# A fused early-fusion block: residual on VectorE, one gate/up bank ahead of the transposes, VectorE's feed-forward queue reordered, attention epsilons inside the sums

## What is computed

```python
h = patch_tokens(x)                        # (32, 36, 256): layernorm, product, layernorm
h = concatenate([h, txt], axis=1)          # (32, 113, 256)
h = h + attention(layernorm(h))            # differential attention, 8 heads, causal
h = h + ffn(layernorm(h))                  # fp4-quantised inputs and weights
# in attention, per head: q, k = rope(rmsnorm(.)); RMS_EPS = eps of float32
#   a = softmax(s[0]) - lam * softmax(s[1]);  out = layernorm(a @ v) * (1 - LAMBDA_INIT), LN_EPS = 1e-5
# in ffn: fp4_linear(silu(fp4_linear(x, w_gate)) * fp4_linear(x, w_up), w_down)
# fp4: per block of 16 elements a scale max|x|/6, then the nearest of 8 magnitudes, times the scale
```

## Time and profile before

| | |
|---|---|
| median of three runs | 659.81 us |
| the profiled execution | 662.52 us, span of its instructions 660.8 us |
| TensorE busy | 576.4 us, 87% |
| VectorE busy | 554.1 us, 84% |
| ScalarE, GpSimd busy | 322.1 us, 309.8 us |
| DMA | 48 GB/s over the span |

### The profile page before, as it was taken

One profiled execution on the slowest core, in us unless ns is written; L12 is line 12 of the kernel. 1 busy time (PEld: TensorE's weight loads), 2 busy tenths in 40 slices (PEclk: granted clock), 3 DMA queues, 4 the chain that ended last, 5 costly groups with the idle time before them and its releaser, 6 DMA issues. The chain is left out here.

```text
span 660.8 us, 14226 instructions
## 1 busy us (share of the span) xinstructions
PE 576.4 (87%) x3666; PEld 470.0 (71%) x3666; DVE 554.1 (84%) x1444; ACT 322.1 (49%) x760; POOL 309.8 (47%) x455
## 2 busy tenths in 40 slices
PE   5665568999999999999999998589999999999996
PEld 4554455767776776777677676478888888888885
DVE  5999847898889889888988985498888888888884
ACT  2242215655665665566565564244544444445442
POOL 2455523555455445545554553155455445545542
PEclk9878776999999999999999997789999999999999
DMA  6900000011111111111111101111111111111111
GB/s 173 325 17 23 24 16 18 27 38 41 30 40 35 35 35 38 40 34 37 35 41 29 42 23 46 30 39 49 48 54 52 54 48 54 49 48 48 57 32 35
DMA packets 33734, 31.99 MB, mean 48 GB/s; under 512 B 6098, under 2 KB 32050, under 8 KB 33714
## 3 DMA queue, kind: packets, MB, share of 16 engines
q1 hardware_dynamic: 33714, 31.75, 16.3%
...
## 5 line engine op out<-in xcount | busy, mean ns | idle before, releaser
L741 PE MATMUL bank<-v_sb,pt 113*113 113x33 f32 x1024 | 109.1, 262 | 0.0
L741 PEld LDWEIGHTS bank<-v_sb,pt 113*113 113x113 f32 x1024 | 108.4, 181 | 0.7 <-issue 0.7
L858 POOL TENSOR_SCALAR_AFFINE_SELECT pt<-pt 113x452 f32<-113x452 f32 x128 | 73.9, 600 | 68.5 <-ACT pt L798 68.5
L798 ACT ACTIVATE pt<-bank 113x452 f32<-113x452 f32 x128 | 63.1, 545 | 38.2 <-PE bank L729 38.2
L138 PE MATMUL bank<-wgu_hi,fx_hi 128*128 128x512 f32 x174 | 69.5, 399 | 8.0 <-DVE fx_lo L1131 8.0
L1177 POOL TENSOR_TENSOR h_deq<-fh,fhb 128x704 f32<-128x704 f32 x29 | 40.3, 1389 | 68.8 <-DVE fhb L1084 56.3
L729 PE MATMUL bank<-q_blk,k_t 64*113 64x452 f32 x256 | 67.7, 605 | 0.0
L138 PE MATMUL bank<-wgu_hi,fx_lo 128*128 128x512 f32 x174 | 66.8, 384 | 0.0
L138 PE MATMUL bank<-wgu_lo,fx_hi 128*128 128x512 f32 x174 | 66.7, 384 | 0.0
L138 PE MATMUL bank<-wqkv_hi,xo_hi 128*113 128x256 f32 (+1 forms) x128 | 50.3, 393 | 17.7 <-DVE xo_lo L923 17.7
L1191 POOL TENSOR_TENSOR fh<-fh,fhb 128x704 f32<-128x704 f32 x29 | 40.3, 1391 | 42.2 <-DVE fhb L1145 42.2
...
## 6 DMA issues: line engine op xcount, KB each, us to landing
...
```

The costliest lines, as they stand in the source:

```text
L741: mm = pe.matmul(pv_ps[s % 2][0:T, s // 2, :], pt[0:T, s, :], v_sb[0:T, s // 2, :], start=True, stop=True, skip_group_check=True)
L798: act.activation(pt[0:T, GS * g:GS * (g + 1), :].rearrange("p s t -> p (s t)"), sc_ps[g % 2][0:T, :], ACT.Exp, scale=1.0 / math.sqrt(HD)). ...
L858: pool.affine_select(out=grp, in_=grp, compare_op=ALU.is_ge, fill=0.0, base=0, pattern=[[0, GS], [1, T]], channel_multiplier=-1).then_inc( ...
```

## The change

It has three parts.

In attention, the epsilons go into the sums as one more element. `v_sb`'s last column, which gives the row sum, is set to sqrt(32 * LN_EPS) in place of 1, so that squaring z with 33 elements a head includes the epsilon. The squares are scaled by 1/HD and 1/VD within the Square, and the q/k squares have a 17th element that holds RMS_EPS. The copy of the row sums, `eps0`, `z_var` and `qk_var` go; `mix` has 4 semaphore steps in place of 5.

In the feed-forward, the residual is no longer multiplied in on TensorE. `rows_out` moves from ScalarE to VectorE and adds the residual `rb` to `down_ps`. Its load is issued one step later.

The queues of the feed-forward get another order: TensorE takes the first gate/up bank, then the transposes of the hidden row, then the other two banks; VectorE takes `x_maxima` and `x_inverse` first and `h_low` after `h_scales`, with `rows_out` at the end; GpSimd takes `x_quotient` ahead of `h_dequantise`; ScalarE `h_magnitude` ahead of `h_high`.

```diff
 LN_EPS = 1e-5
 RMS_EPS = float(np.finfo(np.float32).eps)
+SUM_COLUMN = math.sqrt(VD * LN_EPS)
 LAMBDA_INIT = 0.8 - 0.6 * math.exp(-0.3 * 4)
...
         hr = sb("hr", [P, D])
         xn = sb("xn", [P, D])
         xo_hi, xo_lo = sb("xo_hi", [P, 2 * KD, T], F32R), sb("xo_lo", [P, 2 * KD, T], F32R)
-        sq = sb("sq", [P, 2 * D])
-        ssq = sb("ssq", [P, 2 * SH])
+        sq = sb("sq", [P, 2 * SH, HD + 1])
         NV = 2 + NH + 2 * SH
...
@@ -790,7 +791,8 @@
             def squares(b):
                 act.wait_ge(m["qk_made"], b + 3)
                 after(act, m["qk_sums"], b + 2)
-                act.activation(sq[0:T, :], qk_ps[0:T, :], ACT.Square).then_inc(m["qk_squared"], 1)
+                act.activation(sq[0:T, :, 0:HD], blocks(qk_ps[0:T, :], HD), ACT.Square,
+                               scale=1.0 / math.sqrt(HD)).then_inc(m["qk_squared"], 1)
             def exps(b, g):
                 act.wait_ge(m["scores_made"], NG * b + g + 1)
...
             return steps
         def attention_vector(dve):
-            dve.memset(v_sb[:, :, VD:VD + 1], 1.0).then_inc(m["ones_set"], 1)
+            dve.memset(v_sb[:, :, VD:VD + 1], SUM_COLUMN).then_inc(m["ones_set"], 1)
+            dve.memset(sq[:, :, HD:HD + 1], RMS_EPS).then_inc(m["ones_set"], 1)
+            dve.memset(w1[:, :, VD:VD + 1], 0.0).then_inc(m["ones_set"], 1)
             dve.memset(var[:], 1.0).then_inc(m["ones_set"], 1)
             dve.memset(moments[:], 1.0).then_inc(m["ones_set"], 1)
-            dve.wait_ge(m["ones_set"], 3)
+            dve.wait_ge(m["ones_set"], 5)
             def newton_step(b):
...
                     dve.wait_ge(k["lambda_step"], 5)
                 dve.wait_ge(m["pv_made"], NG * b)
                 dve.reciprocal(rs_1[0:T, :], pv_ps[1][0:T, :, VD]).then_inc(m["mix_step"], 1)
-                dve.tensor_copy(s0[0:T, :], pv_ps[0][0:T, :, VD]).then_inc(m["mix_step"], 1)
-                dve.wait_ge(m["mix_step"], 5 * b - 3)
-                dve.scalar_tensor_tensor(ratio[0:T, :], s0[0:T, :], lam[0:T, :], rs_1[0:T, :], ALU.mult,
+                dve.wait_ge(m["mix_step"], 4 * b - 3)
+                dve.scalar_tensor_tensor(ratio[0:T, :], pv_ps[0][0:T, :, VD], lam[0:T, :], rs_1[0:T, :], ALU.mult,
                                          ALU.mult).then_inc(m["mix_step"], 1)
-                dve.scalar_tensor_tensor(eps0[0:T, :], s0[0:T, :], LN_EPS, s0[0:T, :], ALU.mult,
-                                         ALU.mult).then_inc(m["z_sums"], 1)
-                dve.wait_ge(m["mix_step"], 5 * b - 2)
-                dve.tensor_tensor(blocks(w1[0:T, :], VD), pv_ps[1][0:T, :, 0:VD], spread(ratio[0:T, :], VD),
+                dve.wait_ge(m["mix_step"], 4 * b - 2)
+                dve.tensor_tensor(w1[0:T, :, 0:VD], pv_ps[1][0:T, :, 0:VD], spread(ratio[0:T, :], VD),
                                   ALU.mult).then_inc(m["mix_step"], 1)
-                dve.wait_ge(m["mix_step"], 5 * b - 1)
-                dve.tensor_tensor(blocks(z[0:T, :], VD), pv_ps[0][0:T, :, 0:VD], blocks(w1[0:T, :], VD),
-                                  ALU.subtract).then_inc(m["mix_step"], 1)
+                dve.wait_ge(m["mix_step"], 4 * b - 1)
+                dve.tensor_tensor(z[0:T], pv_ps[0][0:T], w1[0:T], ALU.subtract).then_inc(m["mix_step"], 1)
             def z_sums(b):
                 dve.wait_ge(m["z_squared"], b)
-                dve.tensor_reduce(ssz[0:T, :], blocks(z2[0:T, :], VD), AXX, ALU.add).then_inc(m["z_sums"], 1)
-            def z_var(b):
-                dve.wait_ge(m["z_sums"], 2 * b)
-                dve.scalar_tensor_tensor(var[0:T, HEADS], ssz[0:T, :], 1.0 / VD, eps0[0:T, :], ALU.mult,
-                                         ALU.add).then_inc(m["z_var"], 1)
+                dve.tensor_reduce(var[0:T, HEADS], z2[0:T], AXX, ALU.add).then_inc(m["z_sums"], 1)
             def qk_sums(b):
                 dve.wait_ge(m["qk_squared"], b + 3)
-                dve.tensor_reduce(ssq[0:T, :], blocks(sq[0:T, :], HD), AXX, ALU.add).then_inc(m["qk_sums"], 1)
-            def qk_var(b):
-                dve.wait_ge(m["qk_sums"], b + 3)
-                dve.tensor_scalar(var[0:T, QK], ssq[0:T, :], 1.0 / HD, RMS_EPS, ALU.mult, ALU.add).then_inc(m["qk_var"], 1)
+                dve.tensor_reduce(var[0:T, QK], sq[0:T], AXX, ALU.add).then_inc(m["qk_sums"], 1)
             def residual(b):
@@ -997,7 +990,7 @@
                     between()
                 run(b, seq, (
                     (3, ln_sums), (-1, mix), (1, rope_sum), (-2, residual),
-                    (2, qk_sums), (-1, z_sums), (-2, out_sums), (-1, z_var), (2, qk_var),
+                    (2, qk_sums), (-1, z_sums), (-2, out_sums),
                     ((3, -2), variances)))
...
                 sp.dma_start(xb[:], h2_dram[bass.ds((t + 3) * P, P), :]).then_inc(f["x_loaded"], 16)
             def load_residual(t):
-                after(sp, f["r_added"], t - 1)
-                sp.dma_start(rb[:], h2_dram[bass.ds((t - 1) * P, P), 0:D]).then_inc(f["r_loaded"], 16)
+                after(sp, f["out_made"], t - 2)
+                sp.dma_start(rb[:], h2_dram[bass.ds((t - 2) * P, P), 0:D]).then_inc(f["r_loaded"], 16)
             def store(t):
                 rows = LAST if isinstance(t, int) and t - 2 == FT - 1 else P
@@ -1065,9 +1057,8 @@
             def steps(t):
                 if tile(t, 3):
                     load(t)
-                if tile(t, -1):
+                if tile(t, -2):
                     load_residual(t)
-                if tile(t, -2):
                     store(t)
...
             def scale(amax_of, dst, made):
                 dve.tensor_scalar(dst[:], amax_of, -1.0 / 6.0, -MIN_SCALE, ALU.mult, ALU.min).then_inc(f[made], 1)
+            def rows_out(t):
+                dve.wait_ge(f["down_made"], t - 1)
+                dve.wait_ge(f["r_loaded"], 16 * t - 16)
+                after(dve, f["stored"], 16 * t - 32)
+                dve.tensor_tensor(res[:], down_ps, rb[:], ALU.add).then_inc(f["out_made"], 1)
             def h_low(t):
                 dve.wait_ge(f["ht_high"], t - 1)
@@ -1160,9 +1158,9 @@
             def steps(t):
                 run(t, tile, (
-                    (-2, h_low), (-1, h_rounded), (-1, h_codes), (-1, h_scales), (2, x_maxima), (2, x_inverse),
+                    (2, x_maxima), (2, x_inverse), (-1, h_rounded), (-1, h_codes), (-1, h_scales), (-2, h_low),
                     (0, hidden), (1, x_low), (0, h_maxima), (0, h_inverse), (2, x_rounded), (2, x_codes),
-                    (2, x_scales)))
+                    (2, x_scales), (-2, rows_out)))
             return steps
@@ -1201,7 +1199,7 @@
             def steps(t):
                 run(t, tile, (
-                    (-1, h_dequantise), (2, x_quotient), (0, h_quotient), (2, x_dequantise)))
+                    (2, x_quotient), (-1, h_dequantise), (0, h_quotient), (2, x_dequantise)))
             return steps
@@ -1249,16 +1247,9 @@
                 act.activation(xa[:], xb[:, 0:D], ACT.Identity, bias=xb[:, D:D + 1],
                                scale=xb[:, D + 1:D + 2]).then_inc(f["x_normed"], 1)
-            def rows_out(t):
-                act.wait_ge(f["down_made"], t - 1)
-                after(act, f["stored"], 16 * t - 32)
-                act.activation(res[:], down_ps, ACT.Copy).then_inc(f["out_made"], 1)
             def steps(t):
                 run(t, tile, (
-                    (-2, h_high), (-1, h_magnitude), (0, silu), (1, x_high), (2, x_magnitude), (3, x_norm),
-                    (-2, rows_out)))
+                    (-1, h_magnitude), (-2, h_high), (0, silu), (1, x_high), (2, x_magnitude), (3, x_norm)))
             return steps
...
                 return split3(pe, gu_flat[:, cols], x_hi, x_lo, lambda k: wgu_hi[:, k, cols],
                               lambda k: wgu_lo[:, k, cols], KD)
-            def gate_up(t):
+            def first_columns(t):
                 if isinstance(t, int) and t == 0:
@@ -1282,6 +1273,8 @@
                 pe.wait_ge(f["xt_low"], t + 1)
                 after(pe, f["silu_made"], t)
                 columns(0)
+            def other_columns(t):
                 after(pe, f["hidden_made"], t)
                 columns(1).then_inc(f["gate_made"], 1)
                 columns(2).then_inc(f["up_made"], 1)
...
                     mm = pe.transpose(fxt_ps[:, k * P:(k + 1) * P], x_deq[:, k * P:(k + 1) * P], ident[:])
                 mm.then_inc(f["xt_made"], 1)
-            def residual(t):
+            def down(t):
                 if isinstance(t, int) and t == 2:
                     pe.wait_ge(m["h2_added"], NSEQ)
-                pe.wait_ge(f["r_loaded"], 16 * t - 16)
                 after(pe, f["out_made"], t - 2)
-                pe.matmul(down_ps, ident[:], rb[:], start=True, stop=False).then_inc(f["r_added"], 1)
-            def down(t):
                 pe.wait_ge(f["ht_low"], t - 1)
                 split3(pe, down_ps, lambda k: fh_hi[:, k, :], lambda k: fh_lo[:, k, :],
```

(4 more changed lines are left out.)

27 lines of the change are left out of this document (14 added, 13 removed).

## The result

| | before | after |
|---|---|---|
| median | 659.39 us (4 runs, 658.19 to 660.0) | **676.71 us** (4 runs, 675.53 to 678.23) |
| ratio | | **1.0266**, interval 1.024 to 1.0293 |
| profiled execution (span) | 662.52 (660.8) | 676.38 (674.6) |

Slower, as forecast, but by 2.7% where 1.0% was forecast: 676.7 lies outside the range of 660.5 to 671.5. The two spans differ by 13.8 us. From here on a timeline shows only the rows that bear on its reading.

The account below looks back on a forecast made before the run. Bound: in the feed-forward a 7.75 us VectorE-GpSimd-ScalarE ring, in attention TensorE's ring of 9.60. 26 x 0.20 + 27 x 0.02 + 1.6 - 0.8 = +6.5 us gave a median of 666.3, range 660.5 to 671.5.

Parts of the forecast that it names:

- The ring: Feed-forward tile: VectorE from h_rounded to h_inverse 5.00 us, then via GpSimd and ScalarE to h_rounded 2.75; closed at 7.75.
- TensorE as follower: Feed-forward: TensorE isn't a member of the 7.75 us ring; it waits for h_deq in the same tile.
- the residual: Feed-forward: moving it from TensorE to VectorE's rows_out, inside the wait for h_abs, was put at 0 us.
- The collision: Feed-forward: GpSimd's x_quotient runs across h_rounded's start and shuts it out, 0.20 us a tile in 26 tiles.
- no collision: Feed-forward rival: steps are off by 0.2 us or h_rounded gets in first; +1.3, 661.1 us; chance 0.14.
- full collision: Feed-forward rival: register waits or the loop's branch hold x_inverse back, 0.35 to 0.47 a tile; 670.2 to 673.3; chance 0.12.
- by the queue alone the period is 7.77: VectorE's feed-forward queue: 0.85 us out of the ring, 0.87 in; +0.02 a tile in 27 tiles.
- a rival for attention: Looped attention sequences gain up to 0.24 each, 6 us: 660.3 with the collision, 655.1 without; chance 0.10.
- waits on constants: Attention outside the loop, transposes to xo_high: 0.40 against 0.55 looped, put down to waits on constants, against a gain.
- The tail: Last two tiles: tile 27's down product waits for h_low behind h_scales, the last transposes queue behind it; +1.6 us.
- Attention: Attention edits: 0 us in the 25 looped sequences, -0.8 us from the unrolled ones where the pipeline fills and drains.
- The base: Whole kernel: profiled execution 2.7 us above the median, kept for after: profiled 669.0, median 666.3.

Follow-up runs that it names:

- registers_ahead: The kernel after with GpSimd's order of before and a long-satisfied wait on t - 1 added ahead of h_rounded's and h_magnitude's waits: 667.1 us, 1.0108.
- feed_forward_only: The kernel before with the feed-forward part of the change alone: 677.69 us, 1.0254.
- all_causes_removed: registers_ahead with TensorE's, VectorE's and ScalarE's queues also in the order of before in the last five steps: 665.7 us, 1.0081.

## Why the prediction was wrong in size

**The ring, its members and TensorE as follower** held: taking 0.85 out and putting 0.87 in gives 7.75 outside the loop with GpSimd's order of before, where neither a wait on a register instruction nor the collision is in the way, and the residual on either engine makes no difference in the loop (7.75 both ways).

**The collision** was forecast at 0.20 a tile with a record of about 1.1, and measured at 0.23 with 1.12. Its formula (GpSimd's end plus the instruction's own length less 0.15) fits at two distances to 0.01. `x_quotient` started 2.58 behind `h_inverse`, not 2.48, since its wait too stands on a register instruction (0.16 where the prediction took the 0.07 of `h_quotient`), and `h_rounded` came 0.09 later as well. The rivals "no collision" and "full collision" fall.

**The failed step is "by the queue alone the period is 7.77".** It took the gaps between a release and a start (0.04 at `h_codes`, 0.04 at ScalarE) from the old order, as if they belonged to the instructions. In the loop they depend on who first needs t - 1 in a step, because there the releasing wait lands on the register instruction ahead (0.13 and 0.11 in place of 0.04 twice; with that instruction earlier, in registers_ahead, `h_codes` was back at 0.03). This is 0.16 to 0.17 a tile. With the collision, 0.40 in place of 0.22, and 9.5 us in the stretch of 25 tiles, whose last ones stand outside the loop, in place of 5.5. The earlier trace rows had shown the same thing, 0.40 against 0.55; I set it down as "waits on constants" in a rival for attention and didn't ask which waits the new order would make.

**The tail** was forecast at +1.6 and measured at +6.3. Two things were missed. The x instructions drop out in the last steps, and before the tiles there were only 6.89 and 6.68 long; after, `h_low` stays in the ring and they are 7.75 and 7.55: +1.7. And the products behind the idle time ran at a lower clock: the down product of 27 took 3.5 in place of the 2.2 of the one before it (654.39 to 656.62), the last one 3.9 (668.26 to 672.20) in place of 2.5: +2.8. With the predicted 1.6 that is 6.1 of 6.3. The 1.3 of the product of 27 belong to the orders (seven traces of seven). The 1.5 of the last product belong, as far as is known, to the residual, which the prediction put at 0 us: eight traces of ten with it on VectorE have a slow last product, one of six with it on TensorE.

**Attention** was forecast at -0.8: 0 in the loop held (9.60). The start came 2.0 earlier, of which 0.65 was there by the third `xo_low` (124.09 against 124.74) and some 1.4 came in the drain. The 0.65 is scatter of the front: a kernel with the attention of before (feed_forward_only) has 124.28 there, one with the edits (all_causes_removed) 122.36. The median of the edits alone is 0.3% lower.

**The base.** The prediction carried the 2.7 us by which the profiled execution of before lay above its median over to the kernel after. There the two agree (676.38 and 676.71). So of the 10.4 us that the forecast was short, 7.3 lie in the spans (13.8 against 6.5), 3.7 in the tiles (9.5 where the sum had 5.7) and 4.7 in the tail, less 1.2 in attention, and the other 3.1 in this assumption, which no trace explains.
